# Moving the row-sum matmuls away from the weighted sums in an attention loop, and re-planning the score matmuls around them

## What is computed

```
q, k: 16 half-heads of width 16, rotated by tables;  v: 8 heads of width 32
scores = einsum('bhtd,bhsd->bhts', q, k)          # 16 x 1024 x 1024
probs  = softmax(scores, axis=-1)
probs  = probs.reshape(b, H, 2, t, t)
diff   = probs[:, :, 0] - lam * probs[:, :, 1]
attn   = einsum('bhts,bhsd->bhtd', diff, v)
attn   = attn * rsqrt(mean(attn * attn) + 1e-5) * (1 - LAMBDA_INIT)
```

## Time and profile before

| what | value |
|---|---|
| median of 3 runs | 5198.04 us |
| the profiled execution: its time, its span | 5199.55 us, 5197.8 us |
| mean granted clock of PE, as a share of 2.4 GHz | 0.977 |
| PE busy | 4920.9 us, 95% of the span |
| DVE busy | 3963.6 us, 76% |
| POOL busy | 2929.6 us, 56% |
| ACT busy | 2877.7 us, 55% |
| DMA engines, main queue | 23.4% of their time |

### The profile page before, as it was taken

One profiled execution on the slowest core, in us unless ns is written; L12 is line 12 of the kernel. 1 busy time (PEld: TensorE's weight loads), 2 busy tenths in 40 slices (PEclk: granted clock), 3 DMA queues, 4 the chain that ended last, 5 costly groups with the idle time before them and its releaser, 6 DMA issues.

```text
span 5197.8 us, 67078 instructions
## 1 busy us (share of the span) xinstructions
PE 4920.9 (95%) x24784; PEld 1764.3 (34%) x24784; DVE 3963.6 (76%) x6183; ACT 2877.7 (55%) x5221; POOL 2929.6 (56%) x2118
## 2 busy tenths in 40 slices
PE   6999999999999999999999999999999999999999
PEld 2224242332423333242332424233242333323237
DVE  6977878877787878878887787887778787787525
ACT  1564646556465664646566464665646566463642
POOL 3572737657274664727557273765727466372740
PEclk7899999999999999999999999999999999999999
DMA  6121221303122130222212122230312213022117
GB/s 142 33 59 47 46 64 47 68 29 66 46 46 70 33 74 33 55 61 46 69 33 57 48 46 64 49 67 30 66 46 46 70 33 74 31 51 54 66 49 283
DMA packets 127722, 311.18 MB, mean 60 GB/s; under 512 B 27297, under 2 KB 30498, under 8 KB 113442
## 3 DMA queue, kind: packets, MB, share of 16 engines
q1 hardware_dynamic: 124178, 289.33, 23.4%
q10 hardware_dynamic: 3216, 17.57, 0.9%
HBM read 172.07 MB, written 99.61 MB: 52 GB/s over the span
## 4 chain that ended last, share of the span: by engine, by line
PE 72%; DVE 22%; ACT 4%; issue 1%; POOL 1%; DMA 0%; ACTq 0%; SPq 0%; POOLq 0%; DVEq 0%
PE o_ps L796 15%; PE st L783 14%; PE s_ps L756 14%; PE st L892 11%; DVE neg_max L1044 9%; PE sum_ps L811 7%; PE st L724 4%; DVE swapped L1022 2%; PE st L742 2%; DVE xa L1019 2%; DVE xa L1027 2%; PE st L958 2%; ACT probs L568 1%; DVE xa L1031 1%; PE st L871 1%
## 5 line engine op out<-in xcount | busy, mean ns | idle before, releaser
L475 POOL TENSOR_TENSOR pair_sum<-probs 128x512 f32<-128x512 f32 x2048 | 2833.2, 1417 | 1272.0 <-ACT probs L568 1272.0
L1044 DVE TENSOR_REDUCE neg_max<-s_ps 128x1 f32<-128x512 f32 x4096 | 2592.6, 683 | 803.5 <-PE s_ps L756 800.3
L568 ACT ACTIVATE probs<-st 128x512 f32<-128x512 f32 x4096 | 2153.0, 603 | 1008.2 <-PE st L783 971.0
L756 PE MATMUL s_ps<-k_stack,q_stack 96*128 96x512 bf16 x4096 | 1568.9, 391 | 78.7 <-DVE neg_max L1044 77.2
L783 PE MATMUL st<-q_stack,k_stack 99*128 99x512 bf16 x4096 | 1494.0, 385 | 34.1 <-ACT probs L568 15.9
L796 PE MATMUL o_ps<-probs,values 128*32 128x512 f32 x8192 | 1104.0, 611 | 15.0 <-ACT probs L568 11.8
L783 PEld LDWEIGHTS st<-q_stack,k_stack 99*128 99x128 bf16 x4096 | 370.2, 98 | 1352.9 <-ACT probs L568 823.5
L756 PEld LDWEIGHTS s_ps<-k_stack,q_stack 96*128 96x128 bf16 x4096 | 402.1, 98 | 690.1 <-DVE neg_max L1044 341.4
L811 PE MATMUL sum_ps<-pair_sum,ones 128*32 128x512 f32 x4096 | 534.3, 593 | 9.9 <-DVE o_copy L1088 8.0
L892 PE MATMUL st<-xt,weights 128*128 128x512 f32 x768 | 395.0, 612 | 11.4 <-ACT xt L524 11.4
L515 ACT ACTIVATE probs<-st,gate_bias 128x512 f32<-128x512 f32 x192 | 131.7, 686 | 473.2 <-PE st L892 473.2
(11 more groups left out here) (141 smaller groups left out, 3022.6 us busy)
## 6 DMA issues: line engine op xcount, KB each, us to landing
q_stack<-qk_parts SPq DMA_DIRECT2D x384, 128.0 KB, 4.3
k_stack<-qk_parts SPq DMA_DIRECT2D x378, 128.0 KB, 6.9
swapped<-xa SPq DMA_DIRECT2D x128, 256.0 KB, 2.4
qk_parts<-swapped SPq DMA_DIRECT2D x64, 512.0 KB, 2.8
xa<-in_x SPq DMA_DIRECT2D x16, 1024.0 KB, 6.0
qk_parts<-low_part SPq DMA_DIRECT2D x64, 256.0 KB, 3.0
probs<-in_x SPq DMA_DIRECT2D x16, 1024.0 KB, 9.5
x_rows<-probs SPq DMA_DIRECT2D x16, 1024.0 KB, 3.9
```

What stands on the lines that cost most here:

```text
L475: pool.tensor_tensor(pair_sum[q % 2][:, h, :], probs[a % 4][:, h, :], probs[(a + 1) % 4][:, h, :], ALU.add)\
L568: act.activation(probs[kk % 4][:, h, :], st[n % BANKS][:, :], ACT.Exp).then_inc(exp_done, 1)
L756: pe.matmul(s_ps[i % BANKS][:, :], q_stack[g][0:SROWS, s, t * P:(t + 1) * P], k_stack[g][0:SROWS, s, h * HALF:(h + 1) * HALF], start=True, ...
L1044: dve.tensor_reduce(neg_max2[:, at, i % 2:i % 2 + 1], s_ps[i % BANKS][:, :], AX.X, ALU.max, negate=True).then_inc(max_done, 1)
```

## The change

PE's order in a step becomes: key tile 0, a score, key tile 1, a score, key tile 2, `weighted`, key tile 3, up to two scores, `key_sums` if it is due, the remaining scores. So `key_sums` no longer stands right behind `weighted`: a key tile and up to two scores stand between. The plan of the scores gives the steps that have a `key_sums` a weight of 1.4 instead of 1. Nothing else is touched: the same instructions with the same operands, in another order on PE, and the maxima on DVE distributed over the steps by the new plan.

```diff
+SUM_STEP = 1.4
...
 def score_plan(first, last, g):
+    room = [SUM_STEP if s % 2 == 0 and s >= 4 else 1 for s in range(STEPS)]
     work = WORK[g]
-    per_step = (last - first + sum(work)) / STEPS
+    per_room = (last - first + sum(work)) / sum(room)
     plan, at, due = [], first, 0.0
     for s in range(STEPS):
-        due += per_step - work[s]
+        due += room[s] * per_room - work[s]
         n = max(0, min(int(due), last - at))
...
                     todo = list(plan[s])
-                    for h in range(3):
+                    for h in range(2):
                         key_tile(u, g, s, h)
                         for i in todo[h:h + 1]:
                             score(un, 1 - g, i)
+                    key_tile(u, g, s, 2)
                     if s >= 1:
                         weighted(u, g, s - 1)
+                    key_tile(u, g, s, 3)
+                    for i in todo[2:4]:
+                        score(un, 1 - g, i)
                     if s >= 4 and s % 2 == 0:
                         key_sums(u, g, (s - 4) // 2)
-                    key_tile(u, g, s, 3)
-                    for i in todo[3:]:
+                    for i in todo[4:]:
                         score(un, 1 - g, i)
```

## The result

The changed kernel takes 5240.18 us (median of 5 runs, 5226.47 to 5255.07) against 5198.04: a ratio of 1.0078, with an interval of 1.0053 to 1.0101. The prediction was 5215 with a range of 5185 to 5250 and "slower" as the likeliest case. Direction and range held; the forecast itself was 25 us short of the median.

What follows compares the result with a forecast made beforehand. PE was taken as the bound (busy 95%, 72% of the chain), except where DVE and POOL hold the rotation. Units of +0.9 (16) and +0.4 (15) made 20, the last unit -3: +17, 5215 us against the median; range 5185 to 5250.

Steps and rivals of the forecast that it cites:

- The price: Switches into and out of tiled blocks on PE: each moved key_sums costs 0.23 us, 448 in all, 103 us if unhidden.
- The rival in which the switch costs nothing: PE hides weight loads at the switch, so 16 sums per sequence in B, C, F are free: 5158 us, chance 0.03.
- B: Group 0, steps 11 to 31, PE sets the pace: 10 moved sums, one score more, fewer ACT waits, +1.8 us.
- F: Group 1, steps 22 to 31, PE sets the pace: five moved sums, one score more, shorter waits, +1.0 us.
- the last unit: Final unit, without scores, waiting for ACT: steps with a sum get shorter, 14 x -0.2, -3 us.
- A: Group 0, steps 0 to 10, rotation stage held by POOL's chain: -0.9 us, bounds 0 and -1.3.
- D: Group 1, steps 5 to 11, rotation stage: 1.4 us of waits hide three moved sums, change 0.
- second rival: The long block weighted plus key_sums makes the waits in A, D, E; splitting it gives 5176 us; chance 0.14.
- E: Group 1, steps 12 to 21: later key_sums fills 1.9 us of waits, -0.6 us, bounds -0.8 and +1.2.
- C: Group 1, steps 0 to 4: one moved sum +0.23, one score less -0.22, change 0.
- A at 0: Range case: group 0, steps 0 to 10, gains nothing, all given to new waits; adds 14 us.
- E at its old waits: Range case: group 1, steps 12 to 21, keeps all its waits, +1.2 us; adds 27 us in all.

Runs made afterwards that it cites:

- e8: Kernel before, with only key tile 3 moved ahead of key_sums, scores and plan as before: 5251.10 us beside 5197.45, ratio 1.0102.
- e6: Changed kernel with GpSimd's adds over 256 of 512 columns, the other half of the pair sums constant: 5183.73 us, ratio 0.9973 to the kernel before.
- e7: Kernel before with GpSimd's adds over 256 of 512 columns, the other half of the pair sums constant: 5124.43 us, ratio 0.9858.
- e1: Changed kernel's new order of PE's step with the old plan of scores (SUM_STEP 1.0, not 1.4): 5263.31 us, ratio 1.0125 to the kernel before.
- e2: New plan of scores with the old order, key_sums right behind weighted and third score ahead of both: 5241.19 us, ratio 1.0083 to the kernel before.
- e3: Changed kernel with key_sums put back right behind weighted, plan and score places kept: 5308.92 us, ratio 1.0212 to the kernel before.

## Why the prediction was right, and where not

**The price.** 0.23 us for each moved sum is what the profile after shows (0.32 in, 1.00 out), and e8 shows it with nothing else changed. The rival in which the switch costs nothing fell. The Trainium skill ("TensorE: Matmul & The Clock Gate", Step-by-step: what each phase is for) says that a weight load is pulled ahead when it targets the background weight buffer; the trace shows that between bf16 matmuls and inside the long block, and not at the switches from and to the column-tiled block, where the load starts with its matmul.

**B, F and the last unit** were predicted at +1.8, +1.0 and -3. Measured: +2.2, +0.97, and -4.4 (90.55 to 86.19 us from the unit's first key tile to its last). Key tiles at steps 11, 19 and 27 no longer wait, as said. B's 0.4 too little are small waits that are new or stayed where I had them go: 0.1 for ACT at step 12, 0.1 for DVE at a few steps up to 22, and 0.22 at the second of two neighbouring scores in step 20.

**A** was predicted at -0.9, on the grounds that POOL's chain ends when it did, a little earlier. It ended exactly when it did: the fourth pair is through 29.82 us after the start of A in both. Within the chain the pairs changed. The exponentials of step 6 came 7.87 behind those of step 4 (2046.45 to 2054.32) and not 6.89 (2035.00 to 2041.89), those of step 8 6.24 and not 6.89 behind. The second pair meets three rotation operations that started first and takes 7.90, where it met two and took 6.92; the third takes 5.94 for 6.93. Step 6 got a wait of 1.6 for it, and at step 8 ACT's cast and the second of two neighbouring scores cost the rest. Nothing was won and nothing lost.

**D** was predicted at 0 and is -0.67. I had let the three sums hide in 1.4 us of waits and left 0.7 of them. Those waits were all for ACT, 0.86 at step 9 and 0.42 at step 11 start to start, and with the block split none is left (PE is busy for 19.92 of 19.92). Here the mechanism of the second rival, in which the long block makes the waits, was right. I had put D down to the rotation as well; e6 and e7 show that the adds do not set its length.

**E is the step that failed.** I predicted -0.6, with waits that the later `key_sums` would fill, and bounds of -0.8 and +1.2. It measured +1.35: by the prices 1.9 of waits before and 2.1 after, where I had left 0.1. The 1.2 of them that stood behind ACT's casts and at step 19 were filled as forecast. Those behind POOL and DVE were not. At step 12 `key_sums` still waits 0.28 for the scaling and key tile 3 has a new wait of 0.54, together more than the old 0.51, and step 14 got a wait of 0.82 for POOL's sixth pair that it had not had. POOL's sixth pair, before and after:

```profile
2175.19 6.00 POOL L475 TENSOR_TENSOR pair_sum<-probs 128x512 f32<-128x512 f32 x4
```

```profile
2187.23 6.98 POOL L477 TENSOR_TENSOR pair_sum<-probs 128x512 f32<-128x512 f32 x4
```

I had written of D that no rotation operation is moved; that is so by step, but POOL meets them in time, and this pair now meets two that started first where it met one, for 1 us. The half adds confirm it: without most of POOL's work E is 31.3 us before and 31.4 after, with 0.1 of waits left in the changed kernel as I had said. So what I missed is the part of the waits that POOL and DVE make, 0.7 before and 1.9 after.

**C** was predicted at 0 and is -1.64 in the profiled execution, by the clock alone: with half adds, at a clock of 0.90 and 0.91, C is 17.92 before and 18.02 after.

Summed over a sequence I predicted +1.3. The profile shows +2.2 at the higher clock and would show +3.8 with C at 0. Put into my own sum, the measured A, B, D, E and last unit with C at 0 give about 5253, and with the measured C 5229; the two groups of executions took 5250 to 5255 and 5225 to 5228. So part of the range's success is luck. I had named A at 0 (14 us) and E at its old waits (27 us) as what could go wrong, and both did; D gave 10 back, and the clock of stage C, which was in none of my terms, gave 25 back in the profiled execution. All eight executions at the lower clock took over 5250, outside the range.

**What the sum did not see** is that order and plan are not two terms. Alone they cost 64 and 42 us (e1, e2), together 42. The places of the scores matter as much as those of the sums: with the new plan and joined sums, moving the third score behind key tile 3 costs 68 us (e2 to e3), and taking the sums apart wins that back (5309 to 5240). With the old plan and the sums apart, the new places cost 12 (e8 to e1). The separated sums take the uneven plan better than the even one (5263 to 5240). I had counted the plan as one score moved per unit.

## What to carry to other kernels

Before two blocks on TensorE are moved apart, read start to start what a pair of them costs joined and alone; the difference per move times the number of moves in stages that PE sets is a first estimate of the loss: 16 in a sequence, 57 us, where e8 measured 54. It is not a floor, since a split block can also end waits, as in D and the last unit. Then look at which engine each stage waits for: in a stage held by GpSimd and VectorE, what a PE reordering costs or gains hangs on which operation of the one meets which of the other: nothing in A here, 1.35 us in E. To cure a wait for one engine, move the one instruction that it hangs on, at the steps where it hangs, and leave the rest: that won 21 us here, and at all steps it lost 9.

## What the runs showed of the hardware

A rotation operation of DVE (two float32 inputs in SBUF, 128 x 1024) takes 1.2 us at the least (1.21 at 2054.53 in the kernel before) and up to 2.33 beside POOL's full adds; with adds of half the size 1.23 to 1.74. POOL's adds of 128 x 512 mostly take 1.27 or about 2.26 each, and 1.59 on average in A. The maxima, with one input in PSUM, keep 0.6. The Trainium skill says in "SBUF — State Buffer", Who interferes with whom, that a DVE instruction with two SBUF inputs contends with a GpSimd instruction that reads SBUF; the trace agrees, and it adds that either side can be the one that loses, about 1 us at a time.

One and the same program ran in 5226 or in 5251 us. The windows show the clock of stage C at 1.00 in the profiled execution, and at 0.91 in the same stage of the kernel before and of e6 (0.90 in e7). There PE waits 2.1 us for DVE ahead of one score of step 1 in all of them, and at the lower clock the matmuls behind that wait run at 1.2 GHz instead of 2.4. Timeline of PE in the kernel before, a block of `weighted` that takes 1.06 elsewhere:

```profile
2141.02 1.94 PE L796 MATMUL o_ps<-probs,values 128*32 128x512 f32 x8
```

1.64 us in each of 15 sequences make 25 us, the distance of the groups. No trace of an execution of the group at 5251 was kept, so that its time goes to stage C is inferred from this size and from its mean clock. It need not be stage C in each sequence: in e8, at a mean clock of 0.975, C of this sequence takes 16.75 us. Why an execution falls in one group or the other was not tried.
